# G's mixing product beside K's and V's, and another order of five steps on TensorE

## What is computed

```python
# layer 1: attention with a decaying state, 4 heads, keys of 16, values of 32
delta = shifted(h) - h
x0 = tanh((h + delta * x_proj_mu) @ xl_w1.T) @ xl_w2.T + xl_b2
mus = einsum('btnr,hnr->btnh', tanh(x0).reshape(B, T, 5, 32), x_out_w) + x_bias
r_mu, w_mu, k_mu, v_mu, g_mu = mus                # five mixings
r = (h + delta * r_mu) @ r_w.T                    # and k, v, g, and w through tanh
...
o_t = r_t . S + (r_t . bonus . k_t) v_t           # over the positions t
S = S * w_t + k_t v_t
...
x = layernorm(x + (groupnorm(o) * silu(g)) @ o_w.T)
# layer 2: a shared expert for all rows, and 2 of 16 experts for each row
x = layernorm(x + shared(x) + sum of weight_e * expert_e(x))
```

## Time and profile before

| | us |
|---|---|
| median of 3 runs | 846.95 (846.54 to 847.4) |
| the profiled execution | 840.05 |
| its span, first to last instruction | 838.2 |
| TensorE busy, share of the span | 92% |
| GpSimd busy | 65% |
| VectorE busy | 64% |
| ScalarE busy | 57% |

### The profile page before, as it was taken

How to read it: one execution, slowest core, us unless ns; L and a number is a source line. 1 busy time by engine, 2 the same in 40 slices (tenths; PEclk the granted TensorE clock), 3 DMA queues, 4 the chain that set the end, 5 groups by cost and what they waited for, 6 DMA issues and landing times.

```text
span 838.2 us, 27821 instructions
## 1 busy us (share of the span) xinstructions
PE 773.3 (92%) x8906; PEld 588.8 (70%) x8907; DVE 532.9 (64%) x1714; ACT 479.6 (57%) x1250; POOL 545.6 (65%) x678
## 2 busy tenths in 40 slices
PE   9999999999999999999977759999999999999994
PEld 6666656665566655665555439999999999989741
DVE  4548797777877787678764525555555555555366
ACT  3456666666566655665554305655665665656456
POOL 5565688888888888788886642455554555545444
PEclk9999999999999999999999989999999999999998
DMA  5001111221122202220114512222222222221094
GB/s 175 14 29 43 46 50 38 56 69 49 34 60 65 63 25 60 62 61 26 47 37 128 184 50 72 77 72 62 70 64 61 72 63 60 68 59 44 21 403 189
DMA packets 48271, 61.40 MB, mean 73 GB/s; under 512 B 8594, under 2 KB 33432, under 8 KB 48048
## 3 DMA queue, kind: packets, MB, share of 16 engines
q1 hardware_dynamic: 39200, 42.83, 17.3%
q0 software_dynamic: 8704, 17.06, 6.0%
q10 hardware_dynamic: 272, 0.26, 0.1%
HBM read 37.73 MB, written 23.43 MB: 73 GB/s over the span
## 4 chain that ended last, share of the span: by engine, by line
PE 68%; POOL 13%; issue 9%; ACT 3%; DVE 3%; another core or an unknown queue 2%; SPq 1%; DMA 0%; POOLq 0%; ACTq 0%; DVEq 0%
PE psB L630 16%; PE psO L642 15%; PE psO L559 5%; POOL w_ring L1001 5%; PE psP L342 5%; POOL dispatched_rows L1021 4%; PE psB L501 3%; PE psO L347 2%; PE psP L423 2%; PE psB L491 2%; PE psB L479 2%; PE psP L429 2%; PE psP L619 2%; PE psP L333 2%
## 5 line engine op out<-in xcount | busy, mean ns | idle before, releaser
L1044 POOL DMA_INDIRECT expert_results<-yw_all,row_tail x144 | 147.7, 1026 | 151.8 <-ACT yw_all L914 120.5
L904 ACT ACTIVATE hide<-psB,w_ring 128x128 f32<-128x128 f32 x432 | 126.7, 365 | 85.0 <-DVE hide L1375 44.1
L1021 POOL DMA_INDIRECT dispatched_rows<-rows,slot x128 | 131.0, 1023 | 35.6 <-issue 31.4
L630 PE MATMUL psB<-x1T,w_ring 128*128 128x128 f32 x1152 | 142.3, 277 | 5.2 <-issue 4.6
L642 PE MATMUL psO<-w_sb,hide 128*128 x1152 | 142.6, 277 | 0.5 <-ACT hide L904 0.4
L630 PEld LDWEIGHTS psB<-x1T,w_ring 128*128 128x128 f32 x1152 | 134.2, 192 | 8.6 <-issue 7.9
L642 PEld LDWEIGHTS psO<-w_sb,hide 128*128 128x128 f32 x1152 | 134.2, 192 | 1.0 <-issue 0.9
L1001 POOL TENSOR_TENSOR w_ring<-w_ring,tot 128x128 f32<-128x128 f32 (+2 forms) x160 | 117.6, 754 | 0.0
L1365 DVE COPY w_ring<-w_sb 128x516 f32 x144 | 56.5, 434 | 81.2 <-issue 81.2
L1096 DVE SCALAR_TENSOR_TENSOR psP<-psP,cols,delta 128x512 f32<-128x512 f32 x80 | 57.3, 753 | 54.5 <-PE psP L342 54.5
L863 ACT ACTIVATE hide<-psO,cols 128x512 f32<-128x512 f32 x64 | 44.1, 689 | 62.8 <-PE psO L559 59.3
(11 more groups left out here) (204 smaller groups left out, 1381.4 us busy)
## 6 DMA issues: line engine op xcount, KB each, us to landing
rows<-dispatched_rows SPq DMA_DIRECT2D x144, 66.0 KB
w_sb<-expert_results SPq DMA_DIRECT2D x5, 1024.0 KB, 10.5
h_res<-in_hidden SPq DMA_DIRECT2D x16, 256.0 KB, 3.0
out<-w_sb SPq DMA_DIRECT2D x16, 256.0 KB, 3.4
hT<-in_hidden_t SPq DMA_DIRECT2D x15, 256.0 KB, 4.0
w_sb<-in_w SPq DMA_DIRECT2D x14, 256.0 KB
expert_results<-yw_all,row_tail POOLq DMA_INDIRECT x144
w_sb<-in_w SPq DMA_DIRECT2D x2, 1032.0 KB
```

Source lines behind the costliest of these rows:

```text
L630: last = mm(up_ps(p)[:, c // 2, at:at + PART], w1b[w][s][:, c * 128:(c + 1) * 128], xTe[p][:, s * PART:(s + 1) * PART], start=True, stop=True)
L904: last = A(hide[p][:, c, s * PART:(s + 1) * PART], psB[:, 2 * p + c // 2, at:at + PART], ACT.Relu, bias=w1b[w][s][:, HIDDEN + c:HIDDEN + c ...
L1021: G.indirect_dma_start(rows_dram[:, :], bass.IndirectOffsetOnAxis(slot[u % 2][:, j, k:k + 1], 0), rows[k][u % 2][:, j, :], None).then_inc( ...
L1044: G.indirect_dma_start(back_dram[:, :], bass.IndirectOffsetOnAxis(row_tail[:, i, s, 1:2].bitcast(u32), 0), yw[i][:, s, :], None, bounds_ch ...
```

## The change

Four things on TensorE, none on the other engines, apart from the bank in which Vector finds G's mixing:

- G's mixing product goes to bank 0 of `psB` and right behind K's and V's, ahead of everything that follows them; it waits for `k_tok` of the unit before, whose transposes ScalarE reads from that bank.
- `b_k_tok` goes ahead of `b_o_near`.
- `f_up` 1 goes ahead of `b_kv`, and `f_up` 2 ahead of `a_v`.
- `c_place` goes behind `a_k`.

```diff
-MIX_BANK = {MIX_W: 0, MIX_R: 1, MIX_K: 0, MIX_V: 1, MIX_G: 1}
...
+        mix_ps = {MIX_W: P0, MIX_R: P1, MIX_K: P0, MIX_V: P1, MIX_G: psB[:, 0, :]}
...
-            def a_mix_k_v(u):
+            def a_mix_k_v_g(u):
                 done(pe, "exp_w", u)
                 done(pe, "r_done", u)
                 pe.nop(nofuse=True)
-                mix(P0, MIX_K)
-                mix(P1, MIX_V)
+                mix(MIX_K)
+                mix(MIX_V)
+                before(pe, "k_tok", u)
+                mix(MIX_G)
...
-            def a_mix_g(u):
-                done(pe, f"mixed{MIX_V}", u)
-                mix(P1, MIX_G)
...
             def body(at):
                 at(0, f_up, 0)
+                at(2, b_k_tok)
                 at(2, b_o_near)
-                at(2, b_k_tok)
                 at(3, fill, 5)
-                at(3, a_mix_k_v)
+                at(3, a_mix_k_v_g)
+                at(0, f_up, 1)
                 at(2, b_kv)
-                at(0, f_up, 1)
-                at(0, c_place)
                 at(3, fill, 10, 5, 5)
                 at(3, a_k)
-                at(3, a_mix_g)
+                at(0, c_place)
+                at(0, f_up, 2)
                 at(3, a_v)
-                at(0, f_up, 2)
                 at(2, b_o_far)
                 at(3, a_g)
                 at(1, c_attn)
...
-                ps = unflat(psP[MIX_BANK[n]])
+                ps = unflat(mix_ps[n])
                 V.scalar_tensor_tensor(ps, ps, col(f"x_bias{n}"), delta[:, :, :], ALU.add, ALU.mult).then_inc(sem(f"mul{n}"))
```

More of the change, by code:

```diff
@@ L334, in by_seq, with mix @@
                 return i
-            def mix(ps, n):
+            def mix(n):
                 if n < 4:
@@ L341, in mix @@
                 kw = {"tile_position": (96, 0)} if n == 3 else {}
-                mm(ps, w, a, start=True, stop=True, **kw).then_inc(sem(f"mix_ps{n}"))
+                mm(mix_ps[n], w, a, start=True, stop=True, **kw).then_inc(sem(f"mix_ps{n}"))
             def fill(u, *n):
@@ L383, in a_mix_w_r @@
                 pe.nop(nofuse=True)
-                mix(P0, MIX_W)
-                mix(P1, MIX_R)
+                mix(MIX_W)
+                mix(MIX_R)
             def a_decay_hid(u):
@@ L1106, in a_add @@
                 dve.nop(nofuse=True)
-                V.tensor_tensor(mixed[MIX_BUF[n]][:, :, :], unflat(psP[MIX_BANK[n]]), hT[u % 2][:, :, 1:T + 1], ALU.add).then_inc(sem(f"mixed{n}"))
+                V.tensor_tensor(mixed[MIX_BUF[n]][:, :, :], unflat(mix_ps[n]), hT[u % 2][:, :, 1:T + 1], ALU.add).then_inc(sem(f"mixed{n}"))
             def a_gate(u):
```

## The result

The changed kernel takes 880.88 us (median of 4 runs, 875.29 to 887.83) against 846.75 us before on the same chip: ratio 1.0406, 95% interval 1.0328 to 1.0485. It is slower; the forecast was 841.4 us. The profiled execution took 882.95 us (span 881.1); before it was 840.05 (838.2).

The account below looks back on a forecast made before the run. TensorE was taken as the bound (95% busy in a full round), GpSimd's steps and scatters second. The terms summed to -5.55 us, subtracted from the 846.95 us median for 841.4 us; range 836.0 to 849.0.

Parts of the forecast that it names:

- Term 2: Transposes of K ahead of the near products wait for GpSimd's step 4; cost 0.29 us a round.
- Term 3: TensorE's reorder up to V: K's copy starts between 390.9 and 392.02, V's product between 391.8 and 392.12.
- term 5: GpSimd's step 1 starts 0.27 us behind the second scatter, not 0.78; gain 0.5 us a round, bounds 0 to 1.0.
- Term 1: G's mixing product runs beside K's and V's on TensorE; adds 0 us, bounds 0 to 1.05.
- Term 4: TensorE from V to level 1, without chunk 2: arrives 1.1 us earlier, bounds 0.8 and 1.3.
- rival A: Level 1's completion is held through both scatters even when over before the second; 847.4 us, chance 0.20.
- Term 6: Other rounds: 1 to 12 gain 6.0 us, 0 gains 0.45, -2 and -1 lose 1.2, -3 gains 0.3.
- Rival C: K's copy comes later and delays GpSimd's step 0 by 0.29 us a round; 850.9 us, chance 0.14.

Follow-up runs that it names:

- e12: The kernel before with only the transposes of the keys put ahead of the near products; 883.77 us, ratio 1.0443.
- e15: The changed kernel with state products ahead of chunk 1 again and two 128x128 GpSimd multiplications ahead of the first scatter of 11 rounds; 847.07 us, ratio 0.9999.
- e1: The changed kernel with the state products ahead of chunk 1 again, on the chip with prompt completions; 819.45 us, ratio 0.9967.
- e9: The changed kernel with two more 512-column products ahead of V's wait for K's copy; 872.16 us, ratio 1.0305.
- b1: The kernel before, unchanged, profiled on the same chip as the changed kernel; 846.91 us (one run).
- a1: The changed kernel, unchanged, profiled on the same chip as the kernel before; 879.93 us, ratio 1.038.
- e8: The kernel before with G's mixing beside K's and V's and the transposes ahead of the near products, on a chip with late completions; 887.67 us, ratio 1.0489.
- e6: The changed kernel with the state products ahead of chunk 1 again, on a chip with late completions; 854.06 us, ratio 1.0083.
- e7: The changed kernel with GpSimd's scatters 1 and 2 moved from ahead of step 0 to behind step 2 and scatter 0; 970.24 us, ratio 1.1463.
- e11: The kernel before with GpSimd's power of `o_var` behind scatters 1 and 2 instead of ahead of them; 896.83 us, ratio 1.0631.
- e16: The kernel before with one 128x64 GpSimd multiplication ahead of the first scatter of 11 rounds; 842.31 us, ratio 0.9946.
- e5: The kernel before with G's mixing beside K's and V's and transposes ahead of the near products, on the chip with prompt completions; 820.04 us, ratio 0.9963.
- e13: The kernel of e8 with two small GpSimd multiplications (128x128 and 128x32) ahead of the first scatter of 11 rounds; 852.12 us, ratio 1.0069.

## Why the prediction was wrong

Two steps failed. The one that made the kernel slower is the price of the keys' path in terms 2 and 3: a wait of 0.29 us at face value, and a start of K's copy at 391.63 at the latest, 8.92 us behind the last level. Measured, the copy starts 11.12 us behind it, and step 0 with it 2.2 us later against the scatters. The other, term 5, would have left no gain on such a chip even without that.

**Term 1, G's mixing: right.** Three products take the time of one, 1.07 us in round 11 of after. The Trainium skill, page "TensorE: Matmul & The Clock Gate", section on packing small matmuls, had said so of a pack; the trace agrees.

**Term 2, the transposes: the wait was right, its price was the mistake.** The wait is 0.30 us, forecast 0.29. I let it cost 0.29 us. e12, which does this alone, costs 36.6 us: the state products move from 0.21 to 0.55 us into the first scatter, K's copy comes 1.5 us later against the scatters, and TensorE's idle time ahead of V grows from 0.70 to 1.93 us. I had worked with the same behaviour for level 1, and never asked where the state products stand against a scatter. The rows of before held the answer: their end at 388.25 and the first scatter at 388.04:

```profile
388.04 1.06 POOL L1021 DMA_INDIRECT dispatched_rows<-rows,slot  x1 [0.20 <-issue]
```

**Term 3, the reorder: the step that failed by itself.** I bounded K's copy by "prompt" and "as late as now". It is neither: with chunk 1 ahead, the state products end 1.61 us into the scatters, and K's copy starts 11.12 us behind the last level instead of 8.92. "As late as now" was a bound on a lateness that depends on the place, and I had kept it while I moved the place.

**Term 4** never came to be tried: level 1 starts 18.87 us behind the last level, not 13.9 (before 14.96).

**Term 5, step 1 on GpSimd: wrong on such a chip.** In the changed kernel it wasn't tried either, but e15 has its case, level 1 over before the second scatter of its pair. TensorE and GpSimd there:

```profile
399.20 0.46 PE L457 MATMUL psB<-w_ring,K 64*32 64x64 f32 x32
...
400.20 0.42 PE L457 MATMUL psB<-R_near,K_near 64*32 64x128 f32 x3 [0.23 <-issue]
400.93 0.45 PE L457 MATMUL psB<-R_near,K_near 64*32 64x128 f32 x6 [0.32 <-issue]
401.71 0.54 PE L457 MATMUL psB<-R_near,K_near 64*32 64x128 f32 x16 [0.33 <-issue]
```

```profile
400.18 0.96 POOL L1021 DMA_INDIRECT dispatched_rows<-rows,slot  x1 [0.30 <-issue]
401.97 0.29 POOL L985 TENSOR_TENSOR tot<-tot 128x64 f32<-128x64 f32 x1 [0.83 <-issue]
```

Level 1 ends at 399.66, 0.52 us ahead of that scatter. Its semaphore is raised at 401.84, and step 1 starts 0.83 us behind the scatter and not 0.27; in rounds 1 to 12 of e15 that gap is 0.81 to 0.88. So the 0.5 us a round hung on an overlap that doesn't decide it, and rival A, the completions keep to the scatters, was right here. On the chip with prompt completions step 1 follows the scatter by 0.02 to 0.03 us (e1).

**Term 6.** Round 0, without scatters, gains 0.44 us (13.78 from last level to level 1, against 14.22): forecast 0.45. Rounds -3 to -1 lose 1.2 us net, forecast 0.9. Where there is no scatter, the sum was right to 0.3 us.

**Rival C had the mechanism and the sign**, at 850.9 us. Its size, 0.29 us a round, was that of a delay handed on as it is. Step 0 came 1.0 to 2.2 us later against the scatters, 1.9 us in the mean of rounds 1 to 12: 23 us of the 37.6. The falling clock, which appears in no term and no rival, is worth about 10 us by e9. Some 5 us are left over in these rounds, and 4.6 us behind them (1.1 us between b1 and a1), where after's clock is at half for longer too; I have not taken them apart. That before's one odd round of 28.8 us was a drop of the clock stood in its trace, and I had left it unread.

**Which part costs what**, on chips where before takes 847 us. The exchange of transposes and near products alone: 883.8 (e12). With G beside K and V as well: 887.7 (e8), not more than its runs' spread (881.28 to 898.39) above it. With places and chunk 2 moved as well: 854.1 (e6); by the table they take a completion out from ahead of K's, K's copy comes at 4.4 instead of 5.1 us (no run takes these two parts alone on such a chip without a delay of the scatters), and of the drops of the clock in rounds 1 to 12 one is left. With chunk 1 ahead of the state products as well, the whole change: 880. Costs of parts don't add here.

**Open.** What holds the completions is not settled. Scatters beside them are needed for it (e7, e11), but not enough: in e16 chunk 1, places and K's product end inside the scatters and their semaphores are raised within 0.03 us. In the late cases it nearly always begins with a group of many small products that ends inside a scatter (state products, far products, levels, the transposes behind the near products), or with V's eight, 3.9 to 4.2 us in; what is behind the group is late with it. Whether these products really end late or only their semaphores are raised late, no row can tell: the ends are modelled. But level 0's products in e15 above start in pieces some 0.7 us apart (400.20, 400.93, 401.71), with nothing in the profile that they wait for: there the start itself is held. Why one of the experiments' five chips shows nothing of it is open as well. The changed kernel was not run on that chip; its two nearest relatives took 0.997 and 1.007 of before there.

## What to carry to other kernels

When a step moves in time on one engine, look up what it then overlaps on every other engine, above all a run of GpSimd scatters; a wait seen at one place is no bound for it at another. If a group of small TensorE products ends shortly behind the start of a scatter, a few tenths of a microsecond decide over 1.5 us, and starting the scatters later can be the cheaper half. Take a time from more than one chip before a behaviour like this is built on: 847 and 822 us, and an edit that is 0.4% faster or 4.9% slower, are the same code.

## What was not expected of the hardware

- Semaphores of TensorE's products came late while scatters ran, 6.03 us behind the modelled end in e7's round, and in steps: 1.3, 2.8 and 4.2 us behind the first scatter's start for products that ended at 0.21, 0.55 and 1.61.
- One chip showed none of it: 0.05 us at most for the same products (e5), and the same kernel at 822.5 instead of 847 us.
- In rounds 2 to 12 of after TensorE was idle for 1.6 to 2.3 us ahead of V, and in ten of the eleven a granted clock of 0.50 for 6.8 or 10.2 us came just behind; drops of 3.4 us also came behind 0.8 us (round 1 of after) and 0.7 us (round 9 of before). The idle time alone doesn't decide it. In the changed kernel with 1.9 us of work put there (e9) the clock stayed at 1.00 but for one drop of 3.4 us, and the kernel with more work in it was 8.1 us faster.
- Work added to an engine that is almost the bound made the kernel faster: 35.6 us in e13 against e8 (two chips, before at 847.2 and 846.6 us), 5.3 us in e16 against before.
